# The last layer normalisation of a two-layer graph attention kernel: its apply step moved from VectorE to GpSimd

## What is computed

```
# layer 0: pre-norm attention and MLP
nx = ln(x) * ln1_g + ln1_b
x1 = x + attention(nx, mask=adj, bias=0.1*adj*adj) @ wo + bo
x  = x1 + gelu(ln(x1)*ln2_g + ln2_b @ w1 + b1) @ w2 + b2
# layer 1: attention, residual, post-norm
y   = attention(x, mask=adj) @ Wo + bo + x
mu  = mean(y); var = mean((y - mu)**2)
out = (y - mu) * rsqrt(var + 1e-5) * gamma + beta
```

## Time and profile before

| | |
|---|---|
| time, median of 3 runs | 2329.34 us (2329.33 to 2329.94) |
| the profiled execution: its time, its span | 2329.64 us, 2327.0 us |
| granted TensorE clock, mean | 0.985 |
| PE busy | 2224.4 us, 96% |
| DVE busy | 1949.8 us, 84% |
| ACT busy | 1689.2 us, 73% |
| POOL busy | 1140.1 us, 49% |
| C stage's apply on DVE (L690 on `res_c`) | 128 instructions, 58.4 us |

### The profile page before, as it was taken

How to read it: one execution, slowest core, us unless ns; L and a number is a source line. 1 busy time by engine, 2 the same in 40 slices (tenths; PEclk the granted TensorE clock), 3 DMA queues, 4 the chain that set the end, 5 groups by cost and what they waited for, 6 DMA issues and landing times.

```text
span 2327.0 us, 63225 instructions
## 1 busy us (share of the span) xinstructions
PE 2224.4 (96%) x22336; PEld 1918.5 (82%) x22336; DVE 1949.8 (84%) x8684; ACT 1689.2 (73%) x5646; POOL 1140.1 (49%) x1255
## 2 busy tenths in 40 slices
PE   4799999999999999999999999999999999999986
PEld 4688888888888888888888888888888888888875
DVE  4688888888888888888888888888888888888885
ACT  2577777877777877777777777777777777777773
POOL 0245544555544555544555544555544555554454
PEclk8799999999999999999999999999999999999998
DMA  4011100110101111101010100011100011101000
GB/s 116 19 31 31 38 22 26 36 38 31 38 22 29 33 38 31 38 25 33 26 38 31 38 29 29 27 38 31 37 29 29 27 38 32 37 29 30 16 25 16
DMA packets 94326, 76.02 MB, mean 33 GB/s; under 512 B 8128, under 2 KB 93760, under 8 KB 94016
## 3 DMA queue, kind: packets, MB, share of 16 engines
q1 hardware_dynamic: 94016, 71.99, 10.3%
HBM read 55.20 MB, written 16.78 MB: 31 GB/s over the span
## 4 chain that ended last, share of the span: by engine, by line
PE 45%; ACT 26%; DVE 23%; issue 5%; POOL 0%; POOLq 0%; DVEq 0%; ACTq 0%
PE p_bank L1014 36%; ACT scores L575 20%; DVE normed L798 3%; DVE scores L777 3%; PE p_heads L1109 3%; ACT probs_t L606 3%; DVE stats_M L676 2%; PE p_heads L1095 2%; DVE res_a L856 2%; DVE x_two L690 2%; PE p_bank L1129 2%; PE p_bank L1033 2%; DVE stats_C L676 1%; DVE res_c L856 1%; DVE moments_M L681 1%
## 5 line engine op out<-in xcount | busy, mean ns | idle before, releaser
L575 ACT ACTIVATE scores<-scores,negmax 128x128 f32<-128x128 f32 x2048 | 795.3, 392 | 107.5 <-DVE negmax L777 107.1
L522 POOL TENSOR_TENSOR scores<-scores,inverse 128x512 f32<-128x512 f32 x512 | 543.9, 1067 | 632.5 <-DVE inverse L787 632.5
L575 ACT ACTIVATION_READ_ACCUMULATOR scores<-scores,negmax 128x1 f32 x2048 | 389.3, 190 | 0.0
L1014 PE MATMUL p_bank<-w_down,hidden 128*128 128x256 f32 x3072 | 381.3, 284 | 0.0
L1014 PEld LDWEIGHTS p_bank<-w_down,hidden 128*128 128x128 f32 x3072 | 374.2, 190 | 8.6 <-issue 5.9
L1014 PE MATMUL p_bank<-normed,w_up 128*128 128x512 f32 x1536 | 368.5, 396 | 1.2 <-DVE normed L798 1.1
L1014 PEld LDWEIGHTS p_bank<-normed,w_up 128*128 128x128 f32 x1536 | 283.7, 188 | 66.1 <-issue 7.1
L1109 PE MATMUL p_heads<-ident,scores 128*128 128x128 f32 x2048 | 315.7, 278 | 18.1 <-DVE negmax L777 17.6
L1109 PEld LDWEIGHTS p_heads<-ident,scores 128*128 128x128 f32 x2048 | 237.1, 142 | 52.0 <-DVE negmax L777 41.2
L597 ACT ACTIVATE p_bank<-p_bank,ready_cols 128x512 f32<-128x512 f32 x256 | 169.5, 662 | 130.1 <-PE p_bank L1014 124.5
L1014 PE MATMUL p_bank<-w_o,heads_t 128*128 128x256 f32 x1536 | 248.2, 297 | 3.1 <-DVE heads_t L845 3.1
(11 more groups left out here) (113 smaller groups left out, 3811.9 us busy)
## 6 DMA issues: line engine op xcount, KB each, us to landing
x_in<-in_x SPq DMA_DIRECT2D x32, 512.0 KB, 3.9
res_a<-in_x SPq DMA_DIRECT2D x32, 512.0 KB, 4.1
out<-res_c SPq DMA_DIRECT2D x128, 128.0 KB, 1.8
adj_a<-in_adj SPq DMA_DIRECT2D x32, 256.0 KB, 2.9
adj_c<-in_adj SPq DMA_DIRECT2D x32, 256.0 KB, 2.8
res_c<-in_L_gnn_w SPq DMA_DIRECT2D x1, 512.0 KB, 5.9
values_c<-in_L_gnn_w SPq DMA_DIRECT2D x1, 512.0 KB, 6.7
piece_room<-in_L_gnn_w SPq DMA_DIRECT2D x1, 512.0 KB, 7.8
```

The source lines that it names most:

```text
L522: nc.gpsimd.tensor_tensor(rows_c, rows_c, inverse[:, k % 2, heads].unsqueeze(2).broadcast_to([P, HC, P]), ALU.mult).then_inc(probs_made, 1)
L575: last = nc.scalar.activation(scores[:, k % 2, h], scores[:, k % 2, h], ACT.Exp, scale=-1.0, bias=negmax[:, k % 2, h:h + 1], accum_out=tot ...
L1014: last = nc.tensor.matmul(dst, stationary(i), moving(j), start=(n == 0), stop=(n == total_n - 1))
```

## The change

DVE no longer applies the normalisation of the C stage: in `apply_norm` the branch for C is dropped, and only the rows of stage M are normalised there. POOL does it as the first instruction of `finish`: one `tensor_scalar` with two operands per partition (mean and rstd), a wait for its own completion, then gamma and beta as before. DVE still adds the residual and makes mean and variance.

```diff
@@ -505,6 +505,9 @@
                 _, stage, b = t.unit(r)
                 if stage == "C":
                     unit = t.group(r) * GB + b
+                    pool.wait_ge(rstd_made["C"], unit + 1)
+                    nc.gpsimd.tensor_scalar(res_c[:, b], res_c[:, b], moments["C"][:, b, 0:1], rstd["C"][:, b:b + 1],
+                                            ALU.subtract, ALU.mult).then_inc(ln_applied["C"], 1)
                     pool.wait_ge(ln_applied["C"], unit + 1)
                     nc.gpsimd.tensor_tensor(res_c[:, b], res_c[:, b], gamma[:, :], ALU.mult).then_inc(gained, 1)
@@ -861,9 +864,7 @@
             def apply_norm(t, r):
                 _, stage, b = t.unit(r)
                 group = t.group(r)
-                if stage == "C":
-                    normalize("C", res_c, res_c, b, b + 1, group * GB + b + 1)
-                else:
+                if stage == "A":
                     for b_ in {1: (0, 1), 2: (2,), 3: (3,)}.get(b, ()):
```

## The result

The changed kernel takes 2342.36 us in the median of four runs (2342.02 to 2342.75), against 2329.34 us: a ratio of 1.0058, 95% interval 1.0043 to 1.0073. It is slower by about 13 us, and outside the range I gave. The profiled execution took 2342.18 us with a span of 2340.4 us, 13.4 us more than before.

The account below looks back on a forecast made before the run. PE (96% busy), with waits through PE, ACT and DVE and none on POOL, was taken to bound the kernel. 0 from DVE, 0 in the turns, +2.1 us at the end: 2331.4 us, range 2327.5 to 2336.

Parts of the forecast that it names:

- DVE's relief: Full turns: four instructions removed from DVE in each of 30 turns, 128 in all, 58.4 us; claimed gain 0.
- All four places: Steps 3 to 6 of a turn: each removed DVE instruction is followed by waiting or, in step 6, covered by ACT.
- the upper bound of the new instruction's duration: POOL's new tensor_scalar: at most 0.74 us, from two-input products of 737 ns for 256 columns; 0.65 us was taken.
- The end: Behind the last rstd: three applications now in POOL's line, 3 x 0.73 us less 0.1, so +2.1 us.
- The full turns cost nothing: Steps 3 to 0 of each full turn: POOL's idle times and others' slack take up the added blocks, 0 us.
- The second rival: Step 0: POOL's late C bias holds up DVE's M rows; at c = 1.1, 12.6 us in 30 turns; chance 0.12.
- c: Duration of POOL's new tensor_scalar of 128x256 fp32, taken as 0.65 us, bounded from 0.41 to 0.74 us.
- Covered queues: Full turns: those who wait for POOL's delayed work or for the SP queue have enough slack, so no cost.
- The A bias: Step 5 on POOL: first half would end near 1041.45, DVE's residual needs it at 1042.35; covered by 0.9 us.
- the probabilities of step 6: POOL's first half would end at 1043.7, PE transposes from 1044.77; covered by 1.0 us.
- SP's stores: End of a turn: last store and next adjacency load come up to 1.5 us later; no wait claimed.
- The lock rule: Step 0: two-port VectorE and GpSimd lock each other out for a whole instruction, making POOL's longer queue dangerous; no size.

## Why the prediction was wrong, point by point

- **DVE's relief is worth nothing: right.** All four places were covered as forecast. In step 6 the 0.64 us became 0.61 us of idle time before the inversion, and the kernel with steps 3 and 4 on POOL measures 1.0000.
- **The step that failed is the upper bound of the new instruction's duration**, "One input less should not make it dearer than 0.74 us". It takes 1.23 us, 1.7 times the two-input product, and it isn't DVE that stretches it: at the end of the kernel, with DVE idle, it takes 1.22 us. The bound held the number of inputs for what counts. The runs show that on POOL the form of the instruction counts: 0.37 us fixed and 3.3 ns a column, of which the second operation with its operand makes 1.15. The working of the bound had a fault of the same kind: its 1.2 ns a column and 0.43 us fixed came from two products of different form, gamma with a full second operand and the probabilities with one value per head. The additions of the bias, whose second operand is a row as gamma's is, take 1.29 us for 512 columns, so 2.2 ns a column and 0.18 us fixed. Neither pair gives the new instruction. The Trainium skill ("GPSIMD Engine Reference", Elementwise — side-by-side cycle accounting) gives 1.03 cycles an element for bodies of up to two operations. At its 1.2 GHz the measured column is about 4 cycles, and 2.6 with a single operation, if the fixed part is the same. The measurement decides.
- **The end: right in its place, wrong in its size.** The term was 3 x 0.73 less 0.1. It measured 4.0 us, which is 3 x 1.31 in place of 3 x 0.73; the rstd there took 0.55 us without DVE beside it, as said.
- **"The full turns cost nothing": wrong, as a consequence.** The second rival, with a chance of 0.12, is what happened, and by its own mechanism: the C bias ends at 1056.57, behind the 1056.01 at which DVE's M rows are ready. (What holds them isn't the semaphore that the description of the kernel names; it covers only the first half of the bias for these two rows.) Its point and its price were off, though. I had DVE's rows start at the end of the C bias and the limit at c = 0.89 us. But the path ran already through POOL's product that stood between the two rows, and this had 0.47 us of idle time before it that I left out of the account; and 0.1 us a turn lie under ACT's chain. The slack runs out between c = 1.075 us, at which 28 turns lose 2.6 us in all, and 1.23 us, at which they lose 8.9. At c = 1.23 the rival's formula would have given 0.68 us a turn; it was 0.3, or 8.6 us over the full turns, with 0.8 us in turn 32, where I had put nothing.
- **Covered queues: right.** The A bias, the probabilities of step 6 and SP's stores made nobody wait in the full turns, even at nearly twice the expected price. The cover was of 0.9 us for the A bias, against 0.58 us of additional delay.
- **Not seen at all:** the rstd as a coupling of the blocks. It is free when the blocks of steps 5 and 6 are on the same engine, and costs 32 us over the kernel before when the block of step 5 is moved and that of step 6 is not.

The lock rule of the Trainium skill ("SBUF — State Buffer", Who interferes with whom), which I had weighed, was borne out: DVE's M rows take 0.72 us with POOL kept out, 1.45 with its product between them and 1.75 with the C bias ahead of it, and each stretched row that is named above ends 0.13 to 0.15 us behind the POOL instruction that it met. In the other direction the cost was small here: POOL's product takes 1.14 and 1.10 us beside the rows, and 1.04 without them.

## What to carry to other kernels

An engine that is half idle is not free at every moment: count its idle time between the last point where it is caught up and the next one where somebody waits for it, and compare the sum of what is added there. A cost that no row shows has no upper bound from rows of another form, and two rows give a price by the column only if they have the same form; run the one instruction, or give the range the price at which the slack is used up. And where an engine has an order for two pieces of ready work, the order itself can be worth more than the work: here one wait gave 4.7 us, and the moved 58 us of DVE time gave nothing.

## What the runs showed of the hardware that was not expected

- POOL's `tensor_scalar` on 128x256 fp32 takes 1227 ns with two operations on per-partition operands, 1075 ns with two constants, 934 ns with one operation on a per-partition operand, and 800 ns for 128 columns with both. The `tensor_tensor` of 128x256 takes 738 ns.
- The same application takes 0.38 to 0.41 us on DVE when POOL stays away, and DVE's `scalar_tensor_tensor` with two SBUF inputs takes 0.48 us. A ready DVE instruction of 0.4 us was stretched to 1.38 us behind one half of POOL's bias addition, of 1.32 us.
